# Hybrid attention and feed-forward kernel: the key copy on ScalarE, one normalisation on GpSimd

## The reference, cut to what matters

```python
x = x + attn_a(layernorm(x))      # one head of 1024 features, causal
x = x + ffn(layernorm(x))
x = x + attn_b(layernorm(x))      # 16 heads of 64, causal; ends with its own layer norm, gamma, beta
x = x + ffn(layernorm(x))

# attn_b, for each head:  q = x Wq, k = x Wk, v = x Wv
#   softmax(mask(q k^T / 8)) v, heads joined, @ Wo, y = x + that, y = norm(y) * gamma + beta
# ffn: s = x Win + bin; g = sum_h relu(s * W1[:, h] + b1[:, h]) * W2[:, h] + b2; out = g Wout + bout
```

## Time and profile before

| | us |
|---|---|
| median of three runs | 921.13 |
| the profiled execution | 920.9 |
| its span in the profile | 919.1 |
| TensorE busy over the span | 741.2 |
| VectorE busy | 742.1 |
| ScalarE busy | 541.6 |
| GpSimd busy | 506.5 |

### The profile page before, as it was taken

One profiled execution on the slowest core, in us unless ns is written; L12 is line 12 of the kernel. 1 busy time (PEld: TensorE's weight loads), 2 busy tenths in 40 slices (PEclk: granted clock), 3 DMA queues, 4 the chain that ended last, 5 costly groups with the idle time before them and its releaser, 6 DMA issues.

```text
span 919.1 us, 21221 instructions
## 1 busy us (share of the span) xinstructions
PE 741.2 (81%) x7592; PEld 529.0 (58%) x7592; DVE 742.1 (81%) x1454; ACT 541.6 (59%) x1511; POOL 506.5 (55%) x456
## 2 busy tenths in 40 slices
PE   3476667632899999999999999999999998988942
PEld 2364555522566766666666666666666675656641
DVE  1478888763677788799899979988987998898874
ACT  0257666661566665675677567557656766764643
POOL 2146666443266566556656655665666566556731
PEclk9598877855899998999999999999999999999995
DMA  9111110101199896778878777787778787878740
GB/s 200 43 36 34 58 47 35 43 27 46 37 155 152 146 143 120 133 125 133 139 136 133 140 137 124 132 138 136 131 131 134 131 133 137 142 116 145 133 92 12
DMA packets 367142, 100.29 MB, mean 109 GB/s; under 512 B 347968, under 2 KB 364864, under 8 KB 367040
## 3 DMA queue, kind: packets, MB, share of 16 engines
q1 hardware_dynamic: 363776, 96.86, 59.2%
q10 hardware_dynamic: 3264, 2.10, 0.9%
HBM read 8.73 MB, written 2.10 MB: 12 GB/s over the span
## 4 chain that ended last, share of the span: by engine, by line
PE 41%; DVE 28%; issue 14%; ACT 6%; POOL 4%; SPq 4%; DMA 2%; DVEq 0%; ACTq 0%; POOLq 0%
PE wide L830 10%; DVE ffn_g L1092 5%; DVE prob_hl L946 4%; PE bank L160 4%; PE bank L874 3%; DVE neg_max L958 3%; PE bank L162 3%; PE bank L161 3%; PE bank L194 3%; PE wide L835 3%; PE bank L855 2%; POOL prob_hl L1008 2%; PE bank L857 2%; PE bank L856 2%; DVE ffn_g L421 2%
## 5 line engine op out<-in xcount | busy, mean ns | idle before, releaser
L1008 POOL TENSOR_TENSOR prob_hl<-prob,prob_hl 128x768 f16<-128x768 f32 (+1 forms) x192 | 356.0, 1854 | 260.6 <-DVE prob_hl L946 260.5
L921 ACT ACTIVATE prob<-wide,neg_max 128x128 f32<-128x128 f32 (+3 forms) x512 | 264.5, 527 | 190.9 <-DVE neg_max L958 190.1
L958 DVE TENSOR_REDUCE neg_max<-wide 128x2 f32<-128x256 f32 (+3 forms) x256 | 204.0, 818 | 74.2 <-PE wide L835 73.4
L830 PE MATMUL wide<-k_sb,q_sb 64*128 64x128 f32 (+3 forms) x1024 | 193.7, 476 | 2.6 <-ACT prob L921 1.6
L855 PE MATMUL bank<-v_hi,prob_t 128*128 128x64 f16 x1280 | 133.3, 194 | 26.0 <-DVE ctx_sb L972 17.6
L855 PEld LDWEIGHTS bank<-v_hi,prob_t 128*128 128x128 f16 x1280 | 116.0, 98 | 30.9 <-DVE ctx_sb L972 21.3
L946 DVE CAST prob_hl<-prob 128x768 f16<-128x768 f32 (+1 forms) x192 | 132.9, 692 | 0.6 <-ACT prob L921 0.4
L857 PE MATMUL bank<-v_hi,prob_t 128*128 128x64 f16 x1280 | 133.2, 194 | 0.0
L856 PE MATMUL bank<-v_lo,prob_t 128*128 128x64 f16 x1280 | 133.2, 194 | 0.0
L857 PEld LDWEIGHTS bank<-v_hi,prob_t 128*128 128x128 f16 x1280 | 114.6, 98 | 0.0
L856 PEld LDWEIGHTS bank<-v_lo,prob_t 128*128 128x128 f16 x1280 | 114.5, 98 | 0.0
(11 more groups left out here) (189 smaller groups left out, 1461.2 us busy)
## 6 DMA issues: line engine op xcount, KB each, us to landing
prob_t<-prob_hl SPq DMA_TRANSPOSE x384, 3.1
x_next<-in_L_attn_a_in_features SPq DMA_DIRECT2D x8, 256.0 KB, 3.1
x_attn<-in_L_attn_a_in_features SPq DMA_DIRECT2D x8, 256.0 KB, 3.0
x_sb<-x_done SPq DMA_DIRECT2D x8, 256.0 KB, 2.3
y_res<-bn_y SPq DMA_DIRECT2D x8, 256.0 KB, 2.3
out_x<-x_done SPq DMA_DIRECT2D x8, 256.0 KB, 2.6
wq_a<-in_L_attn_a_w_q ACTq DMA_DIRECT2D x1, 512.0 KB, 5.6
wq_b<-in_L_attn_b_Wq SPq DMA_DIRECT2D x1, 512.0 KB, 8.6
```

Source lines behind the costliest of these rows:

```text
L830: pe.matmul(dst[:, h, c:c + m], q[e, i * P:(i + 1) * P], k[e, 0:m], start=(i == UNIT_ROWS[u][0]), stop=False)
L921: last = act.activation(prob_2[s][:, at:at + m], score_banks(p, s)[:, h, c:c + m], ACT.Exp, bias=neg_max[p % 2][:, h, i:i + 1], accum_out= ...
L958: last = dve.tensor_reduce(neg_max[p % 2][:, :, i:i + 1], score_banks(p, s)[:, :, c:c + m], AX.X, ALU.max, negate=True)
L1008: pool.tensor_tensor(prob_hl[u][:, w:2 * w], prob_2[u][:, 0:w], prob_hl[u][:, 0:w], ALU.subtract)\
```

## The change

The key copy moves from VectorE, where it stood in slot 1 behind the cast, to ScalarE, where it stands in slot 1 behind the exponentials and ahead of the copy of the turned context. The four instructions that apply the last layer norm move from VectorE (pair 5, slot 1) to GpSimd, behind the subtraction of unit 0 of pair 5. There they add a negated mean, for which GpSimd gets one more small product in pair 4, unit 1.

```diff
@@ -805,11 +805,11 @@
             wait(act, "s2", n - 1)
             act.activation(q_sb[p % 2][:, :], QK, ACT.Copy, scale=float(E) ** -0.5).then_inc(sem("q_sb"), 1)
 
-        def keys_vector(dve, b, p):
+        def keys_scalar(act, b, p):
             n = number(b, p)
-            wait(dve, "k_ps", n + 1)
-            wait(dve, "s2", n - 1)
-            dve.tensor_copy(k_sb[p % 2][:, :], QK).then_inc(sem("k_sb"), 1)
+            wait(act, "k_ps", n + 1)
+            wait(act, "s2", n - 1)
+            act.copy(k_sb[p % 2][:, :], QK).then_inc(sem("k_sb"), 1)
 
         def pair_scores(pe, b, p, u):
 
@@ -925,6 +925,8 @@
                     last.then_inc(sem(f"p{s}"), 1)
                 if s == 0 and pair_exists(*later(b, p)):
                     queries_scalar(act, *later(b, p))
+                if s == 1 and pair_exists(*later(b, p)):
+                    keys_scalar(act, *later(b, p))
                 if s == 1 and pair_exists(*earlier(b, p, 2)):
                     wait(act, "ctx_t_ps", n - 1)
                     wait(act, "y_ps", n - 2)
@@ -976,8 +978,6 @@
                     bv, pv = before
                     if 0 <= bv < B - 1:
                         values_vector(dve, bv + 1, pv, MB)
-                if s == 1 and pair_exists(*later(b, p)):
-                    keys_vector(dve, *later(b, p))
                 if s == 1 and p == 2 and 0 <= b - 1 < B:
                     back_sum_vector(dve, b - 1)
                 if s == 2 and p == 2 and 0 <= b - 2 < B:
@@ -992,8 +992,6 @@
                 if s == 1 and p == 4 and 0 <= b - 1 < B:
                     wait(dve, "g_x", b)
                     back_statistics(dve, ffn_norm, lambda i: x_ffn[:, i, :], "gf", b - 1)
-                if s == 1 and p == 5 and 0 <= b - 1 < B:
-                    back_apply_vector(dve, b - 1)
                 if p == 7 and s > 0 and 0 <= b - 1 < B:
                     back_add_vector(dve, b - 1, s - 1)
                 if p < 2 and 0 <= b - 2 < B:
@@ -1073,14 +1071,6 @@
                                                 op0=ALU.mult, op1=ALU.add)
             last.then_inc(sem("g_x"), 1)
 
-        def back_apply_vector(dve, c):
-            wait(dve, "gf_rstd", c + 1)
-            wait(dve, "g_xt_ps", c)
-            for i in range(QB):
-                last = dve.tensor_scalar(ffn_norm.y[:, i, :], x_ffn[:, i, :], ffn_norm.mean_var[:, i, 0:1],
-                                         ffn_norm.rstd[:, i:i + 1], ALU.subtract, ALU.mult)
-            last.then_inc(sem("g_y"), 1)
-
         def back_add_vector(dve, c, j):
             wait(dve, "g_relu", J * c + j + 1)
             if j == 0:
@@ -1114,6 +1104,16 @@
                 back_rstd_gpsimd(pool, y_norm, "gy", c)
             if p == 4 and u == 1:
                 back_rstd_gpsimd(pool, ffn_norm, "gf", c)
+                pool.tensor_tensor(ffn_norm.neg_mean[:, :], ffn_norm.mean_var[:, :, 0], minus_one[:, :], ALU.mult)\
+                    .then_inc(sem("gf_nm"), 1)
+            if p == 5 and u == 0:
+                wait(pool, "gf_rstd", c + 1)
+                wait(pool, "gf_nm", c + 1)
+                wait(pool, "g_xt_ps", c)
+                for i in range(QB):
+                    last = pool.tensor_scalar(ffn_norm.y[:, i, :], x_ffn[:, i, :], ffn_norm.neg_mean[:, i:i + 1],
+                                              ffn_norm.rstd[:, i:i + 1], ALU.add, ALU.mult)
+                last.then_inc(sem("g_y"), 1)
             if p == 4 and u == 2:
                 wait(pool, "g_x", c + 1)
                 wait(pool, "g_done", c)
@@ -1225,6 +1225,7 @@
             for k in range(VSLICES):
                 values_scalar(act, 0, k, VB[k % len(VB)])
             queries_scalar(act, 0, 0)
+            keys_scalar(act, 0, 0)
             over_pairs(act, heads_scalar)
 
         @block.vector
@@ -1234,7 +1235,6 @@
             over_front(dve, front_vector)
             for k in range(VSLICES):
                 values_vector(dve, 0, k, VB[k % len(VB)])
-            keys_vector(dve, 0, 0)
             over_pairs(dve, heads_vector)
 
 
```

## The result

Over 12 runs of each, the changed kernel took 925.62 us (median; 922.89 to 929.27) and the kernel before 921.44 us (918.85 to 923.50). The ratio is 1.005, with a 95% interval of 1.0034 to 1.0067: slower by about 4 us, and clear of no change. The forecast was 925.4 us. The profiled execution took 925.29 us, its span is 923.5 us, 4.4 more than before.

What follows compares the result with a forecast made beforehand. TensorE and VectorE were taken as nearly full, ScalarE as having room. 920.9 - 7.0 - 3.0 - 1.4 - 6.4 + 11.6 + 9.5 + 1.0 = 925.2 us profiled, so 925.4 us forecast; range 914 to 934 us.

Steps and rivals of the forecast that it cites:

- The adds get in ahead: Slot 1, adding pairs: the add begins before GpSimd's subtraction, takes 0.74 us; -7.0 us for sequences 2 to 6, -3.0 last.
- ScalarE's side: Key copy delays the context copy by about 0.5 us; free in 8.93 us pairs, pair 0 gets +0.1 us.
- Pair 3's residual: Residual L1071 in pair 3 begins some 0.2 us earlier, so pair 4 starts sooner: 7 x -0.2 = -1.4 us.
- The normalisation: Pair 5: the four instructions end later on GpSimd, about +1.65 us each in seven sequences, +11.6 us.
- The drain: In the drain the four stand behind L1120 on a chain with no cover: +1.0 us, between 0 and 1.7.
- The rule weighed: Skill's rule on issue order, read as letting GpSimd's queued four run ahead of VectorE's cast; the prediction rejected that reading.
- the fifth rival: Pair 5: GpSimd's four run through ahead of the cast, 7 x 0.4 us less, 922.6 us; chance 0.04.
- The clock: Four of five half-clock lengths leave pair 4, -6.4 us; the clock falls in every sequence's pair 5, +9.5 us.
- the 14 us named for a fall in it: Sign to look for: pair 5 lasts 12.9 us without the clock's fall and over 14 us with it.
- the +21.1 forecast: Pairs 5 and 6, sequences 1 to 7: +11.6 us for later normalised rows and +9.5 us for the clock.
- The -6.4 for pair 4: Pair 4's wait gets 0.2 us shorter and comes at other times, so four of five half-clock lengths go, 1.6 us each.

Runs made afterwards that it cites:

- the swapped order: The changed kernel with the key copy behind the context copy on ScalarE: 923.08 us; with the normalisation also moved to pair 4: 898.16 us.
- fillers: The changed kernel plus 12 unused TensorE matmuls during the wait for the normalised rows in pair 5: 917.90 us, 0.9978 of the kernel before.
- early: The changed kernel with the four normalisation instructions on GpSimd behind pair 4's subtraction of unit 2, ahead of L1120: 899.62 us, 0.9765 of the kernel before.

## Why the prediction was right, point by point

**The adds get in ahead.** Right in mechanism and size: 0.74 us and a subtraction of 2.08, pairs 1 and 2 at 9.73 and 9.81 us where 9.7 and 9.9 were forecast, -7.0 us for sequences 2 to 6 (-2.5 for the last, where 3.0 was taken). The run with the key copy behind the add shows that the order makes it.

**ScalarE's side.** The context copy came 0.46 us later where 0.5 was taken, and pair 0 got 0.15 us longer. In pairs of 8.93 us it cost nothing, as forecast. What I missed is that in pair 1, too, 0.3 us hung on it, as the swapped order shows.

**Pair 3's residual.** Right. It began 10.32 us after that pair's first scores and begins 10.11 after them now (498.62):

```profile
508.73 2.52 DVE L1069 SCALAR_TENSOR_TENSOR x_ffn<-bn_y,yn_rstd,at_y 128x128 f32<-128x128 f32 x4
```

Pair 4 without a length at half clock went from 11.06 to 10.84 us, the 0.2 that was forecast.

**The normalisation.** Right in mechanism, a little too dear. TensorE's idle time in pair 5 was forecast at about 3.4 us and measured 3.04. The forecast for pair 5 at full clock was +1.65 us, 12.9 in all; 12.57 (with fillers) against 10.96 to 11.23 before is +1.3 to 1.6. Of what was taken too much, 0.16 us is the product for the negated mean: it runs in pair 4, and the subtraction that the four follow ended 9.31 us after pair 5's first scores before and 9.19 now. The cast did get in at the start of the four, and cost 0.30 where 0.4 was taken. Doubling and moving the four show the rest: it is a queue position, and VectorE's relief there bought nothing (5.68 us idle). The drain took 0.9 us more where 1.0 was forecast, which is a weak check: with the normalisation on VectorE it took 51.3 to 51.8 us, with it in the changed kernel's place on GpSimd 52.2 to 53.7.

**The rule weighed.** The Trainium skill's "SBUF — State Buffer", section "Who interferes with whom", has issue order decide and the loser wait out the whole instruction. The add at 476.29 (first by 0.16 us) and the subtraction lengthened by 0.44 us agree. Pair 5 agrees too, instruction by instruction: the cast was let in ahead of the four, so GpSimd's full list gave it no lasting hold; the fifth rival is out.

**The clock.** The size came out, the rule behind it did not. +9.5 was forecast and 10.2 was measured, as the difference in pairs 5 and 6 between the changed kernel and the one with fillers, in single executions. As wholes these two differ by 7.4 us, since the one with fillers had three lengths at half clock in pair 4 where the changed kernel had one. I expected the clock to fall in every sequence, and in sequence 1 it held, through a wait of the same 3.04 us:

```profile
363.40:366.90 3.50, 0.46 (x16) 0.34 (x12) 1.82 (x2) 0.12 (x1) 3.50 (x6) 1.00 0.80 153
366.90:370.30 3.40, 3.40 (x45) 2.62 (x46) 0.84 (x2) 2.41 (x6) 1.53 (x1) 1.00 0.54 106
```

TensorE did even less here (0.46 of 3.50 us) than ahead of the fall at 529.4 (0.61 of 3.45). So a stall of this length can bring the clock down, and mostly did, but its length alone does not tell whether it will; what else decides is open. That seven lengths came out, as forecast, is luck: sequence 5 had two. Nor did pair 5 last the 14 us named for a fall in it, but 13.58 at most, with the rest of the loss in pair 6. For the two pairs together the +21.1 forecast and the +21.3 measured agree better than their parts, 11.6 against 11.1 for the later rows and 9.5 against 10.2 for the clock.

The -6.4 for pair 4 is the weakest step. In this execution four of five lengths went, as forecast, but I gave the shorter wait as a reason. The run with the key copy behind the add has pair 4 at 11.08, as long as before, and not one length at half clock there in sequences 1 to 6; the run with fillers has pair 4's shorter wait and three of them. The runs don't tell whether the shorter wait or the moment at which it comes makes the difference, so that part of the match with 925.4 is partly luck. Agreement within 0.2 us means little where runs of one kernel differ by up to 10 us.

## What to carry to other kernels

Before moving work off a full engine, look at what it stands in front of: a short instruction between two that exclude another engine can let that engine in first, and changing the order alone can give the gain: here all of it in the adding pairs, though only 5 of 16.5 us in the whole time, since the copy then came too late for other pairs. Where a result that TensorE needs moves to another engine, read its place in that engine's list: behind 3 us of other work it made a stall and, in most sequences, a fall of the clock; ahead of it there was no stall, and pairs 6 and 7 grew by 7 us, waiting in part for later DMAs. A change of 4 us can be one of -16 and one of +24; run the halves apart, and keep the better one or repair the worse (early, 899.6 us, beats both kernels).

## What the runs showed of the hardware that I had not expected

Twelve matmuls whose result nobody uses, in a stall of 3 us, made this kernel 7 to 8 us faster, by keeping the granted clock at 2.4 GHz behind it. And one kernel's times spread over 918.85 to 923.50 us (before) or 922.89 to 929.27 (after) while its instructions stay the same; the profiles put lengths of 3.4 us at half clock in different pairs of different kernels, each costing 1.4 to 1.6 us where the same pairs without one can be set beside it. Which stall brings one on could not be told from the stall's length: after 3.04 us of waiting the clock fell in most sequences and held in one.
